# Padded broadcast matmuls, C copied among the gelus, a plain scan product, expert products in pairs and a router that normalizes in token order

## The chip, the cores and the metric

One core of a Trainium2 chip runs the whole program. The metric is the device time of one execution in microseconds, as the median of several runs; a lower number is better. Five engines work side by side and meet only at semaphores: TensorE (PE in the profile, with its weight loads as PEld), VectorE (DVE), ScalarE (ACT), GpSimd (POOL) and SyncE (SP), whose queue issues most of the transfers.

## The reference

The input is a batch of 16 images of 64 channels and 256 pixels. Three blocks follow one another, each added to its input. All of it is fp32.

```python
x = x + conv_block(group_norm(x))            # small graph convolution, done once in the prologue
t = tokens(x)                                # 16 x 256 tokens of 64 channels
# selective scan, state 16, inner width 128
z, gate = split(layer_norm(t) @ W_in + b_in)
xc = silu(z @ W_conv + b_conv)
Bp, Cp = split(xc @ W_bc + b_bc)
dt = softplus(xc @ W_dt + b_dt)
h[t] = exp(dt * A) * h[t-1] + dt * xc * Bp ;  y[t] = sum_over_state(h[t] * Cp)
t = t + (y * silu(gate)) @ W_out + b_out
# 8 experts, the best 2 of each token
n = layer_norm(t)
logits = n @ Wr + br ;  weights = top2(softmax(logits)), normalized to sum 1
xe = layer_norm(n) * ln_g[e] + ln_b[e]
out = sum_e weight[e] * (gelu(xe @ W1[e] + b1[e]) @ W2[e] + b2[e])
t = t + out
```

## The kernel before, in words

The 16 images are taken as 8 groups of two images (the two halves of the 128 partitions), so a tile is 128 partitions by 512 tokens. After a prologue (loads, weights brought into shape, group norm, the convolution), a body runs 8 times; a tail then finishes the last group. Body `i` scans group `i` (slots 0 to 7), starts the next two groups (`nxt`, `nxt2`: projections, `dt`, the `B` and `C` products), and finishes the group before (`prev`: output projection, layer norm, router, experts). Every engine has its instructions in an order written by hand, and semaphores say when each may start.

A slot is two blocks of 512 steps. VectorE forms the product of B and the broadcast input `ub` in PSUM (`dve_slot`, line 765), then runs the scan into `hs` (line 772). GpSimd multiplies `hs` by `Cs` (`pool_slot`, line 343), TensorE sums over the state (`pe_sum`, line 1059). After slot 0 of the next body, VectorE gates the sum (`dve_gate`, line 793): this text calls its start the **gate** and counts a body from one gate to the next.

Around slot 1 VectorE finishes the group before: `t1` (line 797), then, once slot 1's scan has been issued, `dve_lnF` (line 803, normalized tokens `tns` for the router), `dve_xn2` (lines 810 and 818, the experts' input) with the first router operations between, and `dve_router2` (lines 834 to 855, about ten operations on 128 x 32 or 128 x 4 elements). Meanwhile GpSimd does slot 0, `step_input` for the next group (lines 328 and 330, 128 x 512 each), slot 1, then `pool_x2` (line 368, the low part of the experts' input), which TensorE needs for the first expert matmul, then five small router operations.

The experts run on TensorE and ScalarE as a chain of eight pairs: matmuls by `W1` (lines 1195, 1196), gelu (line 638), matmuls by `W2` (line 1209). Four broadcasts of the router's weights over the partitions (`pe_wb`, line 1183) are copied to SBUF by ScalarE (line 631). VectorE multiplies each expert's result (bias column added) by its weight (`dve_expert`, line 863, 128 x 256), two after each of slots 4 to 7, and GpSimd adds them up (`pool_acc`, line 355).

## Time and profile before

| what | value |
|---|---|
| median of 3 runs | 400.92 us (400.79 to 401.01) |
| profiled execution | 399.73 us, of which the span of the trace is 398.0 us |
| busy in the span: TensorE, VectorE, ScalarE, GpSimd | 329.9, 333.5, 279.3, 266.2 us |
| prologue and body 0, to the first gate | 94.1 us |
| bodies, gate to gate (7) | 39.0, 38.8, 38.8, 38.8, 38.7, 38.5, 36.9 us |
| tail, from the last gate | 34.5 us |

Busy time is a sum over the span. The three stages have different limits, so what a change is worth is read from the stage that it is in. In the timeline views the first column is the start in us from the start of the span, the second the duration in us.

### The profile page before, as it was taken

What the parts mean: (1) busy time and instruction counts of PE and PEld (TensorE: products, weight loads), DVE (VectorE), ACT (ScalarE), POOL (GpSimd) and SP (SyncE); (2) the same over time, 40 slices, a digit from 0 to 9 for tenths busy, and PEclk for the clock granted to TensorE, in tenths of its full rate; (3) what the DMA queues carried; (4) which work ended last, traced back from release to release, by engine and by line L of the source; (5) the groups of instructions that cost most, each with busy time, mean ns of one, the idle gap of its engine ahead of it and who ended that gap; (6) DMA issues with size and microseconds to landing.
All of it is one profiled execution on the core that took longest, in us unless ns stands there. A gap on an engine that the chain in (4) does not pass through costs nothing. (4 is left out here: it accounts for less than half of the span.)

```text
span 398.0 us, 5484 instructions
## 1 busy us (share of the span) xinstructions
PE 329.9 (83%) x1658; PEld 176.3 (44%) x1658; DVE 333.5 (84%) x454; ACT 279.3 (70%) x458; POOL 266.2 (67%) x270
## 2 busy tenths in 40 slices
...
DMA packets 21236, 59.52 MB, mean 150 GB/s; under 512 B 4924, under 2 KB 13272, under 8 KB 15320
## 3 DMA queue, kind: packets, MB, share of 16 engines
...
q8 instruction: 13, 0.21, 0.3%
...
## 5 line engine op out<-in xcount | busy, mean ns | idle before, releaser
L343 POOL TENSOR_TENSOR hs<-hs,Cs 128x1024 f32<-128x1024 f32 x63 | 149.3, 2373 | 41.8 <-DVE hs L772 41.1
L772 DVE TENSOR_TENSOR_SCAN hs<-av,P 128x1024 f32<-128x1024 f32 x64 | 146.3, 2286 | 4.3 <-POOL av L336 1.3
L638 ACT ACTIVATE hb<-P,b1c 128x512 f32<-128x512 f32 x128 | 81.6, 684 | 17.8 <-PE P L1196 15.3
L765 DVE SCALAR_TENSOR_TENSOR P<-P,bbcol,ub 128x1024 f32<-128x1024 f32 x62 | 79.7, 1285 | 2.5 <-DMA ub<-u_scratch 1.2
L1209 PE MATMUL P<-hb,W2s 128*64 128x256 f32 x512 | 68.7, 391 | 0.0
L1195 PE MATMUL P<-X,W1H 128*128 128x512 f32 x128 | 60.4, 472 | 4.6 <-ACT hb L638 3.7
L1196 PE MATMUL P<-X,W1L 128*128 128x512 f32 x128 | 52.5, 410 | 0.0
L581 ACT ACTIVATE av<-P,Aneg 128x510 f32<-128x510 f32 x68 | 44.1, 688 | 9.4 <-PE P L1148 5.7
L355 POOL TENSOR_TENSOR accs<-accs,mes 128x256 f32<-128x256 f32 x56 | 41.0, 733 | 14.1 <-DVE mes L863 9.5
L1209 PEld LDWEIGHTS P<-hb,W2s 128*64 128x64 f32 x512 | 31.3, 136 | 30.6 <-issue 20.7
L863 DVE SCALAR_TENSOR_TENSOR mes<-P,cols,wbs 128x256 f32<-128x256 f32 x64 | 27.3, 468 | 16.0 <-PE P L1209 9.6
L1148 PE MATMUL P<-D,selD 128*128 128x512 f32 x64 | 33.0, 539 | 6.8 <-ACT av L581 4.3
L581 ACT ACTIVATE av<-av,Aneg 128x510 f32<-128x510 f32 x60 | 38.2, 707 | 0.1
L1195 PEld LDWEIGHTS P<-X,W1H 128*128 128x128 f32 x128 | 25.3, 198 | 27.8 <-ACT hb L638 16.7
L1059 PE MATMUL P<-hs,selS 128*32 128x512 f32 x256 | 30.6, 598 | 5.9 <-POOL hs L343 5.9
L631 ACT ACTIVATE wbs<-P 128x512 f32<-128x512 f32 x32 | 19.1, 598 | 20.7 <-PE P L1183 20.7
L1196 PEld LDWEIGHTS P<-X,W1L 128*128 128x128 f32 x128 | 25.7, 200 | 2.7
L1225 PE MATMUL P<-W1H 128*128 128x512 f32 x53 | 18.2, 449 | 5.2 <-POOL X L368 5.2
L1148 PEld LDWEIGHTS P<-D,selD 128*128 128x128 f32 x64 | 12.2, 196 | 20.7 <-issue 20.3
L1059 PEld LDWEIGHTS P<-hs,selS 128*32 128x32 f32 x256 | 6.8, 109 | 28.0 <-POOL hs L343 15.4
L1183 PE MATMUL P<-wT,selW 32*128 32x256 f32 x64 | 16.1, 330 | 0.0
L360 POOL TENSOR_TENSOR D<-dts,D 64x512 fp32r<-64x512 f32 x8 | 10.1, 1269 | 7.5 <-ACT D L564 6.7
...
## 6 DMA issues: line engine op xcount, KB each, us to landing
...
```

Source lines behind the costliest of these rows:

```text
L343: gp.tensor_tensor(hs[:, at, :, :], hs[:, at, :, :], rep(Cs[:, p, :], 1, 2), ALU.mult).then_inc(S["cm"], 1)
L355: gp.tensor_tensor(acc[:, p, :], prev, mes[:, e % 4, :], ALU.add).then_inc(S["acc"], 1)
L581: a_.activation(steps, dt_of, ACT.Exp, scale=Aneg[:, m:m + 1]).then_inc(S["aexp"], 1)
L638: a_.activation(hb[:, r % 4, :], P[:, (XA, XB)[r % 2], :], ACT.Gelu, bias=b1c[:, r:r + 1]).then_inc(S["gl"], 1)
L765: v.scalar_tensor_tensor(out=ring, in0=rep(P[:, BB, :], 1, 2), scalar=bbcol[:, 0:1], in1=ub[:, 2 * n:2 * n + 2, :], op0=ALU.add, op1=ALU.m ...
L772: v.tensor_tensor_scan(hs[:, (SLOTS * g + n) % RING].rearrange("p a t -> p (a t)"), av[:, 2 * n:2 * n + 2, :].rearrange("p a t -> p (a t)" ...
L863: v.scalar_tensor_tensor(out=mes[:, e % 4, :], in0=P[:, (XC, XD)[e // 2 % 2], HW * (e % 2):HW * (e % 2) + HW], scalar=cols[:, R["b2"] + e: ...
L1059: last = pe.matmul(P[32 * q:32 * q + 32, YS, :], selS[:, k, :], hs[:, (SLOTS * g + n) % RING, q % 2, :], start=(k == 0), stop=(k == 3))
L1148: pe.matmul(P[:, (YS, XA)[m % 2], :], selD[:, m - BY_PE[0], :], D2[:, :], start=True, stop=True).then_inc(S["dt_pe"], 1)
L1195: pe.matmul(P[:, bank, :], W1H[:, e, 128 * k:128 * k + 128], X2[:, :], start=True, stop=False)
L1196: pe.matmul(P[:, bank, :], W1L[:, e, 128 * k:128 * k + 128], X2[:, :], start=False, stop=True).then_inc(S["f1"], 1)
L1209: last = pe.matmul(P[64 * h:64 * h + 64, (XC, XD)[pair % 2], HW * (e % 2):HW * (e % 2) + HW], W2s[:, e, k, :], hb[:, r % 4, HW * h:HW * h ...
```

## The change

Seven edits that touch all five engines:

- **Broadcasts:** `selW` and `wT` get 128 partitions instead of 32 (rows above 32 are zero), so line 1183's matmuls contract over 128 rows.
- **C:** its matmul and its copy to `Cs` move from among the decays to the start of the experts' part, after the second pair of gelus.
- **Scan product:** B's bias goes into PSUM by a matmul of its own (`bhl` by `ones`); line 765 becomes a plain product without a scalar operand.
- **Expert products:** two experts at a time, 128 x 512, on VectorE and GpSimd; a last GpSimd addition folds the two halves.
- **Expert bias:** the weighted sum of `b2` comes from two matmuls per group (`pe_bias`); ScalarE copies it beside `t1`.
- **Logits:** `t1` is multiplied by a centred router matrix `Wrc` at once; `tns`, its two ScalarE operations of 128 x 256 and the bias matmul go.
- **Router norm:** the variance comes per token (`pe_vartok`) as 128 x 4; VectorE scales the logits by it and adds the bias, two operations of 128 x 32, ahead of `dve_xn2`.

In the tail the experts keep the old single form. Four buffers of the prologue move into `mes`.

```diff
...
-        selW = sb("selW", [32, EXP, 128], f32r)
+        selW = sb("selW", [128, EXP, 128], f32r)
...
+        bhl = sb("bhl", [128, ST * BLK], f32r)
+        ones = sb("ones", [128, 64], f32r)
...
-        wT = sb("wT", [32, HW], f32r)
+        wT = sb("wT", [128, HW], f32r)
...
+            sp_.wait_ge(S["k_b2"], 1)
+            for h in range(2):
+                for r in range(2):
+                    sp_.dma_start(b2f[16 * h + EXP * r:16 * h + EXP * r + EXP, 64 * h:64 * h + 64], b2).then_inc(S["ld_b2"], 16)
...
+        def pool_pair(eng, g, p, r):
+
+            eng.wait_ge(S["me"], EXP * g + 2 * r + 2)
+            if r == 0:
+                since(eng, "out_sem", 32 * g)
+                eng.wait_ge(S["bt"], g + 1)
+                prev = t1[:, p:p + 2, :]
+            else:
+                eng.wait_ge(S["acc"], EXP * g + 2 * r)
+                prev = acc[:, :, :]
+            at = 2 * (r % 2)
+            done = gp.tensor_tensor(acc[:, :, :], prev, mes[:, at:at + 2, :], ALU.add)
+            if r < EXP // 2 - 1:
+                done.then_inc(S["acc"], 2)
+            else:
+                done.then_inc(S["acc"], 1)
+                eng.wait_ge(S["acc"], EXP * g + EXP - 1)
+                gp.tensor_tensor(acc[:, 0, :], acc[:, 0, :], acc[:, 1, :], ALU.add).then_inc(S["acc"], 1)
...
+            gp.memset(b2f[:, :], 0.0).then_inc(S["k_b2"], 1)
...
+            gp.memset(bhl[:, :].bitcast(fp32), 0.0).then_inc(S["bhl"], 1)
+            gp.memset(ones[:, :].bitcast(fp32), 1.0).then_inc(S["bhl"], 1)
+            gp.memset(wT[:, :].bitcast(fp32), 0.0).then_inc(S["k_wt"], 1)
...
+            eng.wait_ge(S["ld_b2"], 64)
+            gp.tensor_copy(b2h[:, 0, :], b2f[:, :]).then_inc(S["b2r"], 1)
+            eng.wait_ge(S["b2r"], 1)
+            gp.tensor_tensor(b2h[:, 1, :], b2f[:, :], b2h[:, 0, :], ALU.subtract).then_inc(S["b2r"], 1)
...
-            a_.activation(rs2[:, :], P[:, XB, HW:T], ACT.Ln, bias=epst[:, 0:1]).then_inc(S["ln2"], 1)
+            eng.wait_ge(S["vt"], g + 1)
+            a_.activation(rv[:, 6], P[:, XC, 4 * EXP:4 * EXP + 4], ACT.Ln, bias=epst[:, 0:1]).then_inc(S["ln2"], 1)
...
-            a_.activation(rs2[:, :], rs2[:, :], ACT.Exp, scale=-0.5).then_inc(S["rs2"], 1)
+            a_.activation(rv[:, 7], rv[:, 6], ACT.Exp, scale=-0.5).then_inc(S["rs2"], 1)
...
+        def act_bias(eng, g):
+            eng.wait_ge(S["bt_mm"], g + 1)
+            since(eng, "acc", EXP * (g - 1) + 2)
+            a_.activation(t1[:, 1, :], P[:, XD, HW:T], ACT.Copy).then_inc(S["bt"], 1)
...
                 act_decay(eng, i, 10)
                 if prev is not None:
                     act_lnF2(eng, prev)
-                if nxt is not None:
-                    act_c(eng, nxt, q)
                 act_decay(eng, i, 11)
                 if nxt2 is not None:
                     act_lnA1(eng, nxt2)
-                act_decay(eng, i, 12, 13)
                 if prev is not None:
                     act_router(eng, prev)
+                act_decay(eng, i, 12, 13)
                 if nxt2 is not None:
                     act_lnA2(eng, nxt2)
                 act_decay(eng, i, 14, 15)
                 if prev is None:
                     act_dhi(eng, nxt)
+                    act_c(eng, nxt, q, YS)
                 if prev is not None:
                     a_.preload_act_table_set("gelu_and_others")
                     for n in range(EXP):
                             act_dhi(eng, nxt)
                         if n == 1:
                             act_wt(eng, prev)
+                            if nxt is not None:
+                                act_c(eng, nxt, q, YS)
+                        if n == 2:
+                            act_bias(eng, prev)
                         if n in range(2, 6):
                             act_wb(eng, prev, n - 2)
...
-                v.scalar_tensor_tensor(out=ring, in0=rep(P[:, BB, :], 1, 2), scalar=bbcol[:, 0:1], in1=ub[:, 2 * n:2 * n + 2, :],
-                                       op0=ALU.add, op1=ALU.mult).then_inc(S["bm"], 1)
+                v.tensor_tensor(ring, rep(P[:, BB, :], 1, 2), ub[:, 2 * n:2 * n + 2, :], ALU.mult).then_inc(S["bm"], 1)
...
-        def dve_lnF(eng, g):
-            eng.wait_ge(S["rs2"], g + 1)
-            since(eng, "lg", 2 * g)
-            v.tensor_tensor(tns[:, :], P[:, XB, 0:HW], rs2[:, :], ALU.mult).then_inc(S["tn"], 1)
-
-        def dve_xn2(eng, g, between=None):
+        def dve_xn2(eng, g):
...
-            logits = P[:, XC, 0:4 * EXP].rearrange("p (c e) -> p c e", e=EXP)
-            eng.wait_ge(S["lg"], 2 * (g + 1))
+            logits = rt[:, 2]
+            eng.wait_ge(S["rs2"], g + 1)
+            eng.wait_ge(S["lg"], g + 1)
+            v.tensor_tensor(rt[:, 0], P[:, XC, 0:4 * EXP].rearrange("p (c e) -> p c e", e=EXP), rep(rv[:, 7], 2, EXP), ALU.mult).then_inc(S["lm"], 1)
+            eng.wait_ge(S["lm"], 2 * g + 1)
+            v.tensor_tensor(logits, rt[:, 0], rep(brs[:, :], 1, 4), ALU.add).then_inc(S["lm"], 1)
+            eng.wait_ge(S["lm"], 2 * g + 2)
             v.tensor_reduce(rv[:, 0], logits, AX, ALU.max).then_inc(S["m1"], 1)
...
+        def dve_mes(eng, g, r):
+
+            eng.wait_ge(S["f2"], EXP * KC * g + 2 * KC * (r + 1))
+            eng.wait_ge(S["wb"], EXP // 2 * g + r + 1)
+            since(eng, "acc", EXP * g + 2 * (r - 1))
+            at = 2 * (r % 2)
+            v.tensor_tensor(mes[:, at:at + 2, :].rearrange("p e f -> p (e f)"), P[:, (XC, XD)[r % 2], :],
+                            wbs[:, 2 * r:2 * r + 2, :].rearrange("p e f -> p (e f)"), ALU.mult).then_inc(S["me"], 2)
...
+            v.tensor_copy(bhl[0:1, :], bbx[0:1, :, :].rearrange("p s e -> p (s e)")).then_inc(S["bhl"], 1)
+            eng.wait_ge(S["bhl"], 3)
+            v.tensor_tensor(bhl[32:33, :], bbx[0:1, :, :].rearrange("p s e -> p (s e)"), bhl[0:1, :], ALU.subtract).then_inc(S["bhl"], 1)
...
-                    dve_lnF(eng, prev)
+                    dve_router1(eng, prev)
                     dve_xn2(eng, prev)
                     dve_router2(eng, prev, nxt2)
...
+            pe.matmul(P[:, BB, :], bhl[:, :], rep(ones[:, :], 1, T // 64), start=True, stop=False)
             eng.wait_ge(S["xc"], g + 1)
-            since(eng, "bm", SLOTS * g)
-            pe.matmul(P[:, BB, :], Wrep[:, 0].rearrange("p s e -> p (s e)"), xc[:, g % 2, :], start=True, stop=True).then_inc(S["b_mm"], 1)
-
-        def pe_c(eng, g, bank=XC):
-            if bank == XC:
-                eng.wait_ge(S["sg"], g + 1)
+            pe.matmul(P[:, BB, :], Wrep[:, 0].rearrange("p s e -> p (s e)"), xc[:, g % 2, :], start=False, stop=True).then_inc(S["b_mm"], 1)
...
-            eng.wait_ge(S["cs"], so_far(g, 3))
-            pe.matmul(P[:, XC, 0:4 * EXP], ident[:, :], rep(brs[:, :], 1, 4), start=True, stop=False).then_inc(S["lgb"], 1)
-            eng.wait_ge(S["tn"], g + 1)
+            eng.wait_ge(S["t1"], g + 1)
+            eng.wait_ge(S["wrc"], 1)
             for q in range(2):
-                pe.matmul(P[:, XC, 2 * EXP * q:2 * EXP * q + 2 * EXP], tns[:, 128 * q:128 * q + 128],
-                          Wrt[:, :, :].rearrange("p h e -> p (h e)"), start=False, stop=(q == 1)).then_inc(S["lg"], 1)
+                last = pe.matmul(P[:, XC, 2 * EXP * q:2 * EXP * q + 2 * EXP], t1[:, 2 * (g % 2), 128 * q:128 * q + 128],
+                                 Wrc[:, :, :].rearrange("p h e -> p (h e)"), start=True, stop=True)
+            last.then_inc(S["lg"], 1)
+
+        def pe_vartok(eng, g):
+            eng.wait_ge(S["sq2"], g + 1)
+            for q in range(2):
+                last = pe.matmul(P[:, XC, 4 * EXP + 2 * q:4 * EXP + 2 * q + 2], sq2[:, 128 * q:128 * q + 128],
+                                 avg_m[:, 0:128:64], start=True, stop=True)
+            last.then_inc(S["vt"], 1)
...
+        def pe_bias(eng, g):
+
+            eng.wait_ge(S["wtc"], g + 1)
+            eng.wait_ge(S["b2r"], 2)
+            for r in range(2):
+                last = pe.matmul(P[:, XD, HW:T], b2h[:, r, :], wT[:, :], start=(r == 0), stop=(r == 1))
+            last.then_inc(S["bt_mm"], 1)
...
                     since(eng, "me", EXP * prev)
+                    pe_router(eng, prev)
                     pe_warm(eng, 2, XD)
                     pe_varF(eng, prev)
+                    pe_vartok(eng, prev)
                 pe_spread(eng, i, 11)
-                if nxt is not None:
-                    pe_c(eng, nxt)
                 pe_spread(eng, i, 12)
                 if nxt2 is not None:
                     pe_cenA(eng, nxt2)
-                if prev is not None:
-                    pe_router(eng, prev)
                 pe_spread(eng, i, 13)
                 if nxt2 is not None:
                     pe_varA(eng, nxt2)
                 pe_spread(eng, i, 15)
                 if prev is not None:
                     eng.wait_ge(S["xl2"], prev + 1)
-                    pe_warm(eng, 2, XB)
+                    pe_warm(eng, 1 if nxt is not None else 2, XB)
+                if nxt is not None:
+                    pe_c(eng, nxt)
+                if prev is not None:
                     pe_pair(eng, prev, 0)
                     pe_f1(eng, prev, 2)
                     pe_f1(eng, prev, 3)
                     pe_f2(eng, prev, 1)
                     for n in range(2, 6):
                         pe_pair(eng, prev, n)
+                        if n == 2:
+                            pe_bias(eng, prev)
                         pe_wb(eng, prev, n - 2)
...
```

The order on VectorE in body 1, from slot 1's scan product to the first operation of `dve_router2` (`rt`, `rv`: the router's scratch tiles; `tns`: normalized tokens; `X`: the experts' input), before:

```order
L765 SCALAR_TENSOR_TENSOR P<-P,bbcol,ub 128x1024 [waits scan]
L772 SCALAR_TENSOR_TENSOR hs<-av,P 128x1024 [waits ysum,aexp,bm]
L803 TENSOR_TENSOR tns<-P,rs2s 128x256 [waits rs2]
L810 TENSOR_TENSOR xnt<-P,rqs 64x256 [waits rq]
L810 TENSOR_TENSOR xnt<-P,rqs 64x256
L818 TENSOR_TENSOR X<-P,rqs 64x256
L823 TENSOR_REDUCE rv<-P 128x4 [waits lg]
L826 TENSOR_TENSOR rt<-P,rv 128x32 [waits m1]
L818 TENSOR_TENSOR X<-P,rqs 64x256
L834 SCALAR_TENSOR_TENSOR P<-P,rank 128x32 [waits ex]
```

and now:

```order
L811 TENSOR_TENSOR P<-P,ub 128x1024 [waits scan]
L817 SCALAR_TENSOR_TENSOR hs<-av,P 128x1024 [waits ysum,aexp,bm]
L860 TENSOR_TENSOR rt<-P,rv 128x32 [waits lg,rs2]
L862 TENSOR_TENSOR rt<-rt,brs 128x32 [waits lm]
L864 TENSOR_REDUCE rv<-rt 128x4 [waits lm]
L867 TENSOR_TENSOR rt<-rt,rv 128x32 [waits m1]
L850 TENSOR_TENSOR xnt<-P,rqs 64x256 [waits rq]
L850 TENSOR_TENSOR xnt<-P,rqs 64x256
L854 TENSOR_TENSOR X<-P,rqs 64x256 x2
L875 SCALAR_TENSOR_TENSOR P<-P,rank 128x32 [waits ex]
```

One 128 x 256 operation (`tns`) has gone, two of 128 x 32 have come, and the first four router operations stand ahead of the experts' input instead of within it.

The order on GpSimd from slot 7 of one body to `pool_x2` of the next (`accs`: the experts' sum; `dts`, `rl`: `dt` and the scan's input), before:

```order
L343 TENSOR_TENSOR hs<-hs,Cs 128x1024 [waits scan]
L355 TENSOR_TENSOR accs<-accs,mes 128x256 [waits acc,me] x2
L343 TENSOR_TENSOR hs<-hs,Cs 128x1024 [waits cs,scan]
L328 TENSOR_TENSOR dts<-rl,sp 128x512 [waits dt_out,dlo,sp_relu,sp_ln]
L330 TENSOR_TENSOR rl<-dts,xc 128x512 [waits dt]
L343 TENSOR_TENSOR hs<-hs,Cs 128x1024 [waits scan]
L368 TENSOR_TENSOR X<-xnt,X 64x512 [waits cm,acc,xh2,xn2]
```

and now:

```order
L352 TENSOR_TENSOR hs<-hs,Cs 128x1024 [waits scan]
L366 TENSOR_TENSOR accs<-accs,mes 128x512 [waits acc,me]
L372 TENSOR_TENSOR accs<-accs 128x256 [waits acc]
L352 TENSOR_TENSOR hs<-hs,Cs 128x1024 [waits cs,scan]
L337 TENSOR_TENSOR dts<-rl,sp 128x512 [waits dt_out,dlo,sp_relu,sp_ln]
L339 TENSOR_TENSOR rl<-dts,xc 128x512 [waits dt]
L352 TENSOR_TENSOR hs<-hs,Cs 128x1024 [waits scan]
L396 TENSOR_TENSOR X<-xnt,X 64x512 [waits cm,acc,xh2,xn2]
```

Two additions of 128 x 256 have become one of 128 x 512 and a fold; what follows them is unchanged.

The order on TensorE in the same stretch of body 1, behind the centred `t1` (`sq2s`: its square; line 1137, now 1197: its variance; `W1H`: fillers), before:

```order
L1133 MATMUL P<-t1s,cen_m 128x256 [waits t1]
L1148 MATMUL P<-D,selD 128x512 [waits aexp,dlo]
L1225 MATMUL P<-W1H 128x512 [waits xn1]
L1225 MATMUL P<-W1H 128x512
L1137 MATMUL P<-sq2s,avg_m 128x256 [waits sq2]
L1148 MATMUL P<-D,selD 128x512 [waits aexp,dlo]
L1120 MATMUL P<-xc,Wrep 128x512 [waits t1,sg]
L1148 MATMUL P<-D,selD 128x512 [waits aexp,dlo]
L1065 MATMUL P<-res,cen_m 128x256
L1163 MATMUL P<-brs,ident 128x32 [waits cs]
L1166 MATMUL P<-Wrt,tns 128x16 [waits tn]
L1166 MATMUL P<-Wrt,tns 128x16
```

and now:

```order
L1193 MATMUL P<-t1s,cen_m 128x256 [waits t1]
L1208 MATMUL P<-D,selD 128x512 [waits aexp,dlo]
L1225 MATMUL P<-Wrc,t1s 128x16 [waits wrc,t1,xn1]
L1225 MATMUL P<-Wrc,t1s 128x16
L1302 MATMUL P<-W1H 128x512 x2
L1197 MATMUL P<-sq2s,avg_m 128x256 [waits sq2]
L1232 MATMUL P<-avg_m,sq2s 128x2 [waits sq2]
L1232 MATMUL P<-avg_m,sq2s 128x2
L1208 MATMUL P<-D,selD 128x512 [waits aexp,dlo] x2
```

The two router matmuls (lines 1166, now 1225) have moved from behind `tns` to ahead of the variance, and the variance per token (line 1232) stands behind it; C's matmul (line 1120) has left the stretch.

## Rows read from the trace of the kernel before

**Rows 1.** Windows, one body: stretch, length, busy PE, PEld, DVE, ACT, POOL, clock, DMA

```profile
171.80:210.60 38.80, 34.49 (x182) 17.45 (x182) 37.31 (x46) 33.67 (x57) 30.98 (x28) 1.00 0.79 181
```

**Rows 2.** Timeline of VectorE, the body that begins at 210.60

```profile
210.60 0.69 DVE L793 TENSOR_TENSOR ygs<-P,sg 128x512 f32<-128x512 f32 x1 [0.18 <-PE P L1059]
...
213.76 2.29 DVE L772 TENSOR_TENSOR_SCAN hs<-av,P 128x1024 f32<-128x1024 f32 x1
215.97 0.42 DVE L803 TENSOR_TENSOR tns<-P,rs2s 128x256 f32<-128x256 f32 x1
216.31 0.86 DVE L810 TENSOR_TENSOR xnt<-P,rqs 64x256 f32<-64x256 f32 x2
...
217.98 0.19 DVE L826 TENSOR_TENSOR rt<-P,rv 128x32 f32<-128x32 f32 x1
...
218.95 0.20 DVE L834 SCALAR_TENSOR_TENSOR P<-P,rank 128x32 f32<-128x32 f32 x1 [0.32 <-ACT P L620]
...
221.06 1.28 DVE L765 SCALAR_TENSOR_TENSOR P<-P,bbcol,ub 128x1024 f32<-128x1024 f32 x1
```

**Rows 3.** Timeline of GpSimd, the same body

```profile
209.38 1.60 POOL L355 TENSOR_TENSOR accs<-accs,mes 128x256 f32<-128x256 f32 x2
...
214.65 1.27 POOL L330 TENSOR_TENSOR rl<-dts,xc 128x512 f32<-128x512 f32 x1
216.13 2.36 POOL L343 TENSOR_TENSOR hs<-hs,Cs 128x1024 f32<-128x1024 f32 x1 [0.21 <-DVE hs L772]
218.76 1.27 POOL L368 TENSOR_TENSOR X<-xnt,X 64x512 fp32r<-64x512 f32 x1 [0.28 <-DVE X L818]
```

**Rows 4.** Timelines of GpSimd and VectorE, the last body

```profile
334.74 1.26 POOL L368 TENSOR_TENSOR X<-xnt,X 64x512 fp32r<-64x512 f32 x1 [0.23 <-POOL hs L343]
...
335.58 0.47 DVE L846 TENSOR_TENSOR rt<-rt,rv 128x32 f32<-128x32 f32 x1
```

**Rows 5.** Timelines of the prologue: VectorE, GpSimd, SyncE's queue

```profile
11.55 1.57 DVE L882 TENSOR_TENSOR gdev<-mv,gmean 128x8 f32<-128x8 f32 x1
...
13.54 2.09 POOL L440 TENSOR_TENSOR ub<-av 128x256 f32<-128x256 f32 x3 [0.44 <-DMA av<-in_L_conv_Wr]
...
20.22 0.29 SPq L302 DMA_DIRECT2D ub<-in_L_ffn_ln_b  x1
...
29.03 3.69 POOL L447 TENSOR_TENSOR wbs<-hb,cols 128x2048 f32<-128x2048 f32 x1 [11.14 <-DMA hb<-in_L_ffn_W]
...
29.37 3.39 DVE L944 TENSOR_SCALAR Aneg<-Aexp 128x16 f32<-128x16 f32 x1
```

**Rows 6.** Timelines of ScalarE and TensorE around the router, body at 210.60

```profile
214.79 0.47 ACT L589 ACTIVATE rs2s<-P,epst 128x256 f32<-128x256 f32 x1 [0.21 <-PE P L1137]
...
214.82 1.02 PE L1120 MATMUL P<-xc,Wrep 128*128 128x512 f32 x2
...
217.12 0.60 PE L1166 MATMUL P<-Wrt,tns 128*128 128x16 f32 x4
```

**Rows 7.** VectorE groups by line and form: busy, mean ns | idle before

```profile
L760 DVE TENSOR_TENSOR P<-P,hs 128x1024 f32<-128x1024 f32 x2 | 2.5, 1233 | 4.2 <-PE P L1159 4.2
```

**Rows 8.** Timeline of VectorE, a pair of expert products after slot 4

```profile
197.48 0.85 DVE L863 SCALAR_TENSOR_TENSOR mes<-P,cols,wbs 128x256 f32<-128x256 f32 x2
```

**Rows 9.** Timelines of ScalarE and VectorE, slot 7 ahead of the gate at 210.60

```profile
205.24 1.33 ACT L581 ACTIVATE av<-av,Aneg 128x510 f32<-128x510 f32 x2
...
208.14 2.29 DVE L772 TENSOR_TENSOR_SCAN hs<-av,P 128x1024 f32<-128x1024 f32 x1
```

**Rows 10.** Timeline of TensorE in the tail

```profile
382.00 0.50 PE L1183 MATMUL P<-wT,selW 32*128 32x256 f32 x2
382.43 0.51 PE L1195 MATMUL P<-X,W1H 128*128 128x512 f32 x1
382.77 0.40 PE L1196 MATMUL P<-X,W1L 128*128 128x512 f32 x1
```

**Rows 11.** Line 846 in all bodies: ns of the shortest, the median, the longest

```profile
L846 DVE TENSOR_TENSOR rt<-rt,rv x8: 180/182/465, 104.0 to 373.4; 128x32 f32<-128x32 f32 x8
```

More of the change, by code:

```diff
@@ L59 @@
 bm scan cm ysum
-yg po t1 cen2 sq2 var2 ln2 rs2 lnq rq tn xn2 xh2 xl2
-lg lgb m1 dd ex s1 ms1 o1 e2 m2 s2 s2r ms2 o2 den rden num wt wn vhi vlo wtr wtc wb_mm wb
+yg po t1 cen2 sq2 var2 ln2 rs2 lnq rq xn2 xh2 xl2
+lg vt lm wrc m1 dd ex s1 ms1 o1 e2 m2 s2 s2r ms2 o2 den rden num wt wn vhi vlo wtr wtc ld_b2 k_b2 b2r bt_mm bt wb_mm wb
 f1 gl f2 me acc out_sem""".split()
@@ L164, in build @@
         ygs = sb("ygs", [128, T])
-        t1 = sb("t1s", [128, 2, HW])
+        t1 = sb("t1s", [128, 3, HW])
+        b2h = sb("b2h", [128, 2, 128], f32r)
         sq2 = sb("sq2s", [128, HW])
-        rs2 = sb("rs2s", [128, HW])
         rqs = sb("rqs", [128, HW])
-        tns = sb("tns", [128, HW])
         xnt2 = sb("xnt2", [64, T])
@@ L465, in weighted @@
                     if prev is not None:
-                        for e in range(lo, lo + 2):
-                            pool_acc(eng, prev, q, e)
+                        pool_pair(eng, prev, q, lo // 2)
                 if i == 0:
@@ L603, in act_lnF2 @@
             eng.wait_ge(S["var2"], g + 1)
-            since(eng, "tn", g)
+            since(eng, "dd", g)
             since(eng, "xn2", 2 * g)
@@ L719, in _ @@
             eng.wait_ge(S["b_mm"], 1)
-            a_.activation(B0, P[:, BB, :], ACT.Identity, bias=bbcol[:, 0:1]).then_inc(S["b0"], 1)
+            a_.activation(B0, P[:, BB, :], ACT.Copy).then_inc(S["b0"], 1)
             act_lnA1(eng, 1)
@@ L810, in dve_xn2 @@
                 v.tensor_tensor(xnt2[:, HW * h:HW * h + HW], P[q, XB, 0:HW], rqs[q, :], ALU.mult).then_inc(S["xn2"], 1)
-            if between is not None:
-                between()
             since(eng, "f1", EXP * KC * g)
@@ L815, in dve_xn2 @@
                 q = slice(64 * h, 64 * h + 64)
-                if h == 1 and between is None:
-                    dve_router1(eng, g)
                 v.tensor_tensor(X2[0:64, HW * h:HW * h + HW], P[q, XB, 0:HW], rqs[q, :], ALU.mult).then_inc(S["xh2"], 1)
         def dve_router1(eng, g):
-            logits = P[:, XC, 0:4 * EXP].rearrange("p (c e) -> p c e", e=EXP)
-            eng.wait_ge(S["lg"], 2 * (g + 1))
+            logits = rt[:, 2]
[5 more added lines that the diff above has]
+            eng.wait_ge(S["lm"], 2 * g + 2)
             v.tensor_reduce(rv[:, 0], logits, AX, ALU.max).then_inc(S["m1"], 1)
@@ L1132, in pe_cenF @@
             since(eng, "gl", EXP * KC * g)
-            pe.matmul(P[:, XB, 0:HW], cen_m[:, :], t1[:, p, :], start=True, stop=True).then_inc(S["cen2"], 1)
+            pe.matmul(P[:, XB, 0:HW], cen_m[:, :], t1[:, 2 * p, :], start=True, stop=True).then_inc(S["cen2"], 1)
         def pe_varF(eng, g):
```

62 lines of the change are left out of this document (41 added, 21 removed).

## Prediction

> **What bounds the kernel now.** First the windows of one body, then VectorE's and GpSimd's timelines inside it. In 38.80 us from gate to gate VectorE is busy 37.31, TensorE 34.49, ScalarE 33.67, GpSimd 30.98 [rows 1]. VectorE's row has only two gaps that its neighbours cause: 0.18 us at the gate, where TensorE's sum of slot 7 comes late, and 0.32 us ahead of the router's first masked operation (line 834), which waits for ScalarE's exponentials [rows 2]. So seven bodies go at VectorE's pace, and a change is worth there what it adds to or takes from VectorE's chain between two gates. I count from the gate at 210.60: slot 1's scan starts at +3.16, its next operation at +5.37, and slot 2's product, P(2), at +10.46 [rows 2].
>
> At the gate GpSimd arrives last: after slot 7's second pair of additions (1.60 us) it is directly in slot 0's product, then `dt` and `u`, then slot 1's product at +5.53, then `pool_x2`, which ends at +9.43 and releases the experts [rows 3].
>
> **A wait that the trace already has.** In the last body one small VectorE operation, line 846 (128 x 32, both inputs in SBUF), took 0.47 us from 335.58 and ended at 336.05. GpSimd's `pool_x2` ran from 334.74 to 336.00 [rows 4]. Line 826 is of the same size with one input in PSUM, ran from 217.98, in the middle of GpSimd's slot 1 (216.13 to 218.49), and took 0.19 [rows 2, 3]. The prologue repeats it: line 882 (both inputs in SBUF, 128 x 8) took 1.57 and ended at 13.12, as GpSimd's copies ended (13.54 less the 0.44 idle: 13.10); line 944 (another form, all in SBUF) took 3.39 and ended at 32.76, GpSimd's line 447 ended at 32.72 [rows 5]. I read: such a VectorE operation stands still until GpSimd has an idle moment. The Trainium skill, "SBUF — State Buffer", section "Who interferes with whom", states it so: a VectorE instruction with two SBUF inputs contends with a GpSimd instruction that reads SBUF, and whichever starts first holds the shared ports to its end, while one with at most one SBUF input does not contend. The rows agree, and the rule speaks against this change.
>
> **The change in a body.** The new `dve_router1` has two operations of that kind where there was none: line 862 (logits plus `brs`) and line 867 (less the maximum; its first input was in PSUM before). Both stand directly behind slot 1's scan, where GpSimd hardly rests.
>
> When does it begin? Before, ScalarE's first operation on the variance started at 214.79 [rows 6]. Now two router matmuls stand ahead of the variance (0.60 for the old pair [rows 6]) and two more behind it, while ScalarE's two operations per token shrink to four columns. I put `rs2` at +5.85, 0.5 behind the scan.
>
> When is GpSimd busy? Its last pair now costs 1.27 (the duration of 128 x 512 in `u`) plus a fold of 0.80 (half of the 1.60) against 1.60, so +0.47. Of that the 0.21 idle ahead of slot 1 [rows 3] takes some: slot 1 runs from about +5.85 to +8.2.
>
> So line 862 reaches the port as that product begins, and waits to +8.27. Then the maximum, and line 867 ends at +8.7. Experts' input: two of 0.43 and two of 0.43 (1.73 in all [rows 2]), to +10.4; by then the exponentials are ready, and the 0.32 wait is gone. Behind it `dve_router2` takes 2.11 as now (218.95 to 221.06 [rows 2]): P(2) at +12.44 instead of +10.46, **+1.98**. The 0.42 of `tns` and two small operations are in this sum. `pool_x2` ends 2.33 later, at +11.76.
>
> **What the body gets back.** The product without the scalar operand: the only plain 128 x 1024 product with one PSUM input in the trace took 1233 ns [rows 7], line 765 takes 1.28 [rows 2], so 0.05 each. A pair of expert products: 0.85 for two of 128 x 256 [rows 8]; one of 128 x 512 from PSUM takes 0.69 (line 793 [rows 2]), so 0.16 each. To slot 5's scan that is four products and one pair, **-0.36**. From there the later chain is GpSimd's, since it is what the gate waits for: two pairs from 1.60 to 1.28 each, **-0.64** (VectorE saves as much there: three pairs 0.48, three products 0.15). Sum per body +1.98 - 0.36 - 0.64 = **+0.98**, times 7 = **+6.9**. Bounds: line 862 gets into the pause between `u` and slot 1 (then only line 867 waits, +1.53 instead of +1.98), or neither waits (5.85 + 0.7 for four small operations + 1.73 + 2.11 = +10.39, so -0.07).
>
> **Experts.** C's matmul (1.02 [rows 6], less one filler dropped, 0.24) now stands ahead of the first expert matmul, its copy and the bias copy among the gelus (my estimate 0.47 for both, part of them in ScalarE's waits): with `pool_x2` the experts come 2.33 + 0.78 + 0.47 = 3.6 later. Before, the last decays ended at 206.57, 1.57 ahead of slot 7's scan [rows 9], and that scan itself now comes 1.98 - 0.30 (six products) - 0.48 (three pairs) = 1.2 later: 2.8 may be lost. So the sides are level if the broadcasts save 0.8. A broadcast pair with 32 rows, two of 256 columns, takes 0.43 from its start to the next; the expert matmul of 512 columns and 128 rows behind it takes 0.34 [rows 10]. Of the two the operand with fewer rows is the dearer, so I let padding halve the broadcasts: four times 0.2, and this part costs nothing. Without the saving it costs 0.8 a body if every term adds, 0.35 if the copies hide behind gelus. The Trainium skill, "TensorE: Matmul & The Clock Gate", section "Why this matters for your kernels", speaks against the saving: a single matmul with K = 32 takes the same time as one with K = 128. No row here has both shapes at one width, so that is a rival below.
>
> **Ends.** Prologue: about 0.64 us of new fills on GpSimd (my estimate for their 128 x 512 elements and some more, between 0.2 and 1) close the 0.44 pause ahead of line 440 in which line 882 got through, so it falls behind line 440 (2.09 [rows 5]), up to +2.7 on the group norm. Four more transfers on SyncE's queue at 0.3 [rows 5] delay line 447 by 1.2, and what waits behind it on VectorE (line 944). These overlap: I take **+2.0**, bounds +0.2 (both beside other loads) and +3. Body 0: six products, **-0.2**. Tail: router's two operations +0.44, later variance +0.4, `tns` -0.34, broadcasts down to -0.8 that mostly hide behind gelus: **+0.1**.
>
> **Sum.** 2.0 - 0.2 + 6.9 + 0.1 = +8.8. The profiled execution took 399.73, 1.2 below the median, so 408.5 in a profile and **409.7** as a median.
>
> **Rivals.**
> - *No wait (faster).* If a 128 x 32 operation gets its inputs between GpSimd's reads, P(2) comes at +10.4 and a body gains 1.07: 7 x -1.07 + 1.9 (the ends) = -5.6, **395.3**. For it: line 846 took 0.18 as a median [rows 11]; against: in the body of rows 2 and 3 it ran after `pool_x2`, with GpSimd idle, and the instance with GpSimd at work took 0.47. It decides where P(2) comes less than 0.73 later (7 x -0.27 + 1.9 = 0). Chance 0.14.
> - *One of two waits.* Line 862 slips into the pause ahead of slot 1; +0.53 a body, 3.7 + 1.9 = +5.6: **406.5**. Chance 0.14.
> - *The experts become the bound.* Padding saves nothing; the decays of slot 7 come late by 0.6, between 0.35 and 0.8, and a body costs 1.58: x 7 + 1.9 = +13.0, **413.9**. Chance 0.14.
> - My forecast: 0.54. The last 0.04 is a mixture near zero.
>
> Measurement of this kernel tells apart about 0.2%. The forecast and the two middle rivals are slower, the first rival faster: faster 0.15, same 0.03, slower 0.82. The likeliest case alone spans 407.5 (prologue at its lower bound) to 411.5. The range goes to 404.0, between the partial wait and a body that hides part of it, and to 414.5 for the experts' case.
>
> **What would show it.** Lines 862 and 867 with about 2 us between them instead of 0.2 each, one ending as GpSimd's slot 1 (now line 352) ends; P(2) at gate + 12.4; bodies of about 39.8; pairs of products at 0.69, products at 1.23, additions at 1.28; broadcasts at 0.2 to 0.25 a pair. If lines 862 and 867 take 0.19 in the bodies, the forecast is wrong in sign. If they wait but bodies are no longer, another engine already set P(2).

## Result, and the profile after

| what | before | changed |
|---|---|---|
| median of 6 runs | 400.97 us | 414.32 us (411.61 to 415.78) |
| ratio, 95% interval | | 1.0324 (1.0302 to 1.0347) |
| profiled execution, span | 399.73, 398.0 us | 411.61, 409.9 us |
| first gate | 94.1 us | 96.9 us |
| gate to gate (7) | 39.0, 38.8, 38.8, 38.8, 38.7, 38.5, 36.9 us | 40.7, 39.4, 40.4, 40.3, 39.4, 39.6, 38.4 us |
| tail, from the last gate | 34.5 us | 34.8 us |

The kernel is 3.2% slower. Of the 11.9 us in the span, 2.8 come before the first gate, 8.9 in the seven bodies, 0.3 in the tail. The profiled execution is the fastest of the six, 2.7 us below their median. Ahead of the last body, three bodies take 39.4 to 39.6 and three 40.3 to 40.7. One of the four executions in experiment 5 below took 1021.92 us, for a reason that no row shows, and the ratio there leaves it out.

The timeline of VectorE in the body that begins at 177.01 (start, duration, operation), for comparison with [rows 2]:

```profile
183.06 0.19 DVE L860 TENSOR_TENSOR rt<-P,rv 128x32 f32<-128x32 f32 x1 [0.66 <-ACT rv L633]
183.29 1.89 DVE L862 TENSOR_TENSOR rt<-rt,brs 128x32 f32<-128x32 f32 x1
...
185.44 0.19 DVE L867 TENSOR_TENSOR rt<-rt,rv 128x32 f32<-128x32 f32 x1
...
189.46 1.23 DVE L811 TENSOR_TENSOR P<-P,ub 128x1024 f32<-128x1024 f32 x1
```

and of GpSimd, for [rows 3]:

```profile
175.79 1.28 POOL L366 TENSOR_TENSOR accs<-accs,mes 128x512 f32<-128x512 f32 x1
177.16 0.73 POOL L372 TENSOR_TENSOR accs<-accs 128x256 f32<-128x256 f32 x1
...
182.78 2.35 POOL L352 TENSOR_TENSOR hs<-hs,Cs 128x1024 f32<-128x1024 f32 x1
187.45 1.26 POOL L396 TENSOR_TENSOR X<-xnt,X 64x512 fp32r<-64x512 f32 x1 [2.32 <-DVE X L854]
```

Line 862 is as small as line 860, which has its first input in PSUM and takes 0.19. It takes 1.89 and ends at 185.18; GpSimd's slot 1 ends at 185.13. No wait is shown in brackets: the engine counts as busy while it stands. Behind it everything is late: P(2), line 811, starts 12.45 behind the gate instead of 10.46, and `pool_x2` (line 396) ends at +11.70 instead of +9.43; GpSimd, which held VectorE up, then idles 2.32 waiting for it. In the whole trace:

```profile
L862 DVE TENSOR_TENSOR rt<-rt,brs x8: 191/1454/1941, 103.0 to 383.1; 128x32 f32<-128x32 f32 x8
```

(shortest, median, longest, in ns). The shortest is that of the tail, where GpSimd is idle.

The savings are there too, in the groups by line and form (busy us, mean ns of one):

```profile
L811 DVE TENSOR_TENSOR P<-P,ub 128x1024 f32<-128x1024 f32 x62 | 76.0, 1226 | 2.7 <-DMA ub<-u_scratch 0.7
L366 POOL TENSOR_TENSOR accs<-accs,mes 128x512 f32<-128x512 f32 x21 | 27.0, 1285 | 2.4 <-DVE mes L914 2.4
L914 DVE TENSOR_TENSOR mes<-P,wbs 128x512 f32<-128x512 f32 x28 | 18.6, 666 | 0.0
```

**Why two kinds of body.** Windows of two bodies, and of the stretch from +10 to +16 in each (length, busy PE, PEld, DVE, ACT, POOL, then the granted clock as a share of full speed):

```profile
257.69:297.07 39.38, 33.86 (x186) 17.79 (x186) 36.67 (x43) 33.95 (x60) 30.18 (x24) 1.00 0.76 172
177.01:217.44 40.43, 35.06 (x186) 18.64 (x186) 37.93 (x43) 32.45 (x57) 31.60 (x26) 0.96 0.78 176
267.69:273.69 6.00, 4.57 (x18) 2.40 (x20) 5.73 (x16) 5.59 (x10) 2.68 (x7) 1.00 1.01 220
187.01:193.01 6.00, 4.47 (x10) 2.42 (x10) 5.76 (x15) 4.23 (x8) 2.46 (x6) 0.72 1.01 223
```

In the longer one TensorE runs for some time at 0.50, the lower of its two levels (1.2 GHz), just when the experts should begin. Its timeline there shows what it did before and during the fall:

```profile
186.61 1.05 PE L1208 MATMUL P<-D,selD 128*128 128x512 f32 x2 [1.60 <-ACT av L616]
188.76 0.80 PE L1302 MATMUL P<-W1H 128*128 128x512 f32 x1 [1.10 <-POOL X L396]
189.36 1.91 PE L1180 MATMUL P<-xc,Wrep 128*128 128x512 f32 x2
```

Two pauses, 1.60 for ScalarE's decays (ScalarE waits for the router, line 867, ahead of them) and 1.10 for `pool_x2`; then C's matmul takes 1.91, against 1.02 at full clock [rows 6]. The pauses alone do not tell which body has the fall: they are 0.44 and 1.12 in the body at 257.69, which kept full clock, and 0.45 and 1.11 in a body of experiment 6 (at 258.27) which did not and took 40.89 instead of 39.38. Why the clock falls in one and not in the other stays open. What the fall costs is seen at the body's end, on VectorE:

```profile
214.96 2.29 DVE L817 TENSOR_TENSOR_SCAN hs<-av,P 128x1024 f32<-128x1024 f32 x1 [0.75 <-PE P L1115]
```

The next body's first scan waits for TensorE's sums (line 1115), which stand behind the experts in TensorE's queue. The bodies at 96.89 and 177.01 have this wait of 0.75, that at 217.44 one of 0.84 for ScalarE's decays; those at full clock wait only 0.26, at the gate. The sixth body, of 39.6, had a fall too (0.56 in the mean from +10 to +16) without such a wait; it has no `nxt2` to start. The body of before that begins at 210.60 has a fall of the clock too, and the same length as the others:

```profile
210.60:249.37 38.77, 35.73 (x182) 18.18 (x182) 37.33 (x47) 33.42 (x56) 30.95 (x28) 0.96 0.78 179
```

There VectorE waits 0.18 at the gate and at most 0.1 in the 27 us ahead of it. I read: there the experts' slack paid for the fall, and `pool_x2`, 2.0 to 2.3 later, has used that slack up.

### The profile page after: what moved, and what is told of

Its sections match the earlier page's. It is cut to its first block and busy times, and to the rows that moved or that the text cites. A ratio compares the mean times of both kernels' runs of the same rounds, so it can differ in the third digit from the quotient of the medians.

```text
span 409.9 us, 5566 instructions
## 1 busy us (share of the span) xinstructions
PE 336.8 (82%) x1691; PEld 185.8 (45%) x1691; DVE 331.3 (81%) x437; ACT 274.5 (67%) x465; POOL 267.8 (65%) x255
## 5 line engine op out<-in xcount | busy, mean ns | idle before, releaser
L811 DVE TENSOR_TENSOR P<-P,ub 128x1024 f32<-128x1024 f32 x62 | 76.0, 1226 | 2.7 <-DMA ub<-u_scratch 0.7
L1272 PE MATMUL P<-X,W1L 128*128 128x512 f32 x128 | 53.4, 417 | 0.0
L1208 PE MATMUL P<-D,selD 128*128 128x512 f32 x64 | 29.9, 514 | 25.6 <-ACT av L616 23.7
L1208 PEld LDWEIGHTS P<-D,selD 128*128 128x128 f32 x64 | 12.2, 206 | 40.1 <-issue 39.8
L366 POOL TENSOR_TENSOR accs<-accs,mes 128x512 f32<-128x512 f32 x21 | 27.0, 1285 | 2.4 <-DVE mes L914 2.4
L1302 PE MATMUL P<-W1H 128*128 128x512 f32 x46 | 16.7, 462 | 7.2 <-POOL X L396 7.2
L396 POOL TENSOR_TENSOR X<-xnt,X 64x512 fp32r<-64x512 f32 x7 | 8.8, 1264 | 16.2 <-DVE X L854 16.2
L914 DVE TENSOR_TENSOR mes<-P,wbs 128x512 f32<-128x512 f32 x28 | 18.6, 666 | 0.0
L904 DVE SCALAR_TENSOR_TENSOR mes<-P,cols,wbs 128x256 f32<-128x256 f32 x8 | 3.5, 480 | 16.1 <-PE P L1286 8.8
```

The lines of the kernel that those rows point to most:

```text
L366: done = gp.tensor_tensor(acc[:, :, :], prev, mes[:, at:at + 2, :], ALU.add)
L811: v.tensor_tensor(ring, rep(P[:, BB, :], 1, 2), ub[:, 2 * n:2 * n + 2, :], ALU.mult).then_inc(S["bm"], 1)
L1208: pe.matmul(P[:, (YS, XA)[m % 2], :], selD[:, m - BY_PE[0], :], D2[:, :], start=True, stop=True).then_inc(S["dt_pe"], 1)
L1272: pe.matmul(P[:, bank, :], W1L[:, e, 128 * k:128 * k + 128], X2[:, :], start=False, stop=True).then_inc(S["f1"], 1)
L1302: pe.matmul(P[:, bank, :], W1H[:, 0, 0:128], W1H[:, 0:2, :].rearrange("p e f -> p (e f)"), start=True, stop=True)
```

## Experiments

Ratios are to the kernel before on the same chip, with the 95% interval.

**1. The two router tiles in PSUM (e1_psum).** Only the place of two tiles changes.

```diff
+        scaled = P[:, XC, 160:160 + 4 * EXP].rearrange("p (c e) -> p c e", e=EXP)
+        biased = P[:, XC, 192:192 + 4 * EXP].rearrange("p (c e) -> p c e", e=EXP)
...
-            logits = rt[:, 2]
+            logits = biased
...
-            v.tensor_tensor(logits, rt[:, 0], rep(brs[:, :], 1, 4), ALU.add).then_inc(S["lm"], 1)
+            v.tensor_tensor(logits, scaled, rep(brs[:, :], 1, 4), ALU.add).then_inc(S["lm"], 1)
```

> Two intermediate tiles of the router (scaled logits, logits with bias) lie in PSUM instead of SBUF, so that neither line 862's nor line 867's counterpart has two inputs in SBUF; number, size and order of all operations stay. Theory (the wait is for GpSimd, because of two SBUF inputs): both operations take 0.19 to 0.2 us, P(2) comes at gate + 10.5 to 10.8 instead of 12.2 to 12.45, pool_x2 ends 1.5 earlier, bodies of 37.8 to 38.3, time 398 to 402. Rival (what holds P(2) is the late variance rs2 and the order of the operations): P(2) stays at + 11.5 or later and the time above 409.

399.1 us, ratio 0.9949 (0.9928 to 0.997): 15 us less than the changed kernel. VectorE's and GpSimd's timelines in one body (line 864 was 862):

```profile
179.90 0.20 DVE L864 TENSOR_TENSOR P<-P,brs 128x32 f32<-128x32 f32 x1
```

```profile
179.38 2.36 POOL L354 TENSOR_TENSOR hs<-hs,Cs 128x1024 f32<-128x1024 f32 x1
```

It now runs in 0.20 in the middle of GpSimd's slot 1. Ahead of the last body P(2) comes at +10.6 to +11.6, later than expected where the variance is late (the counterpart of line 860 starts at +5.9 to +6.9); these bodies take 37.9 to 38.8, up to 0.5 more than expected.

**2. One operation added to the kernel before (e5_ss, e6_ps).** Unused output, directly behind line 803; the second kernel differs in one input.

```diff
             v.tensor_tensor(tns[:, :], P[:, XB, 0:HW], rs2[:, :], ALU.mult).then_inc(S["tn"], 1)
+            v.tensor_tensor(rt[:, 2], rank[:, :, :], rank[:, :, :], ALU.add)
```

```diff
+            v.tensor_tensor(rt[:, 2], P[:, XB, 0:4 * EXP].rearrange("p (c e) -> p c e", e=EXP), rank[:, :, :], ALU.add)
```

> The kernel before with one operation more per group on VectorE, directly behind line 803: 128 x 32, both inputs the constant tile rank in SBUF, output unused. Nothing waits for it but VectorE's own order. Theory (it stands still until GpSimd's product of slot 1 has ended): it takes 1.8 to 2.2 us in the bodies, P(2) comes 1.5 to 2.0 later and pool_x2 2 later, bodies longer by 1.2 to 2.5 (nothing is given back here), time 408 to 418. Rival (small operations slip through): it takes 0.2, time 401 to 402.5.

> The same added operation with one of its two inputs in PSUM (the centred tokens, in a bank that is free to read there), otherwise the kernel before. Theory: 0.2 us, P(2) 0.1 to 0.2 later, time 401 to 402.5. Rival (any added operation here costs a stall): as the other kernel.

Two inputs in SBUF: 414.28 us, 1.034 (1.0294 to 1.0386). One in PSUM: 400.54 us, 1.0001 (0.9973 to 1.003). The added line in all groups of the first and of the second:

```profile
L804 DVE TENSOR_TENSOR rt<-rank x8: 183/1777/2226, 100.3 to 382.8; 128x32 f32<-128x32 f32 x8
```

```profile
L804 DVE TENSOR_TENSOR rt<-P,rank x8: 180/180/181, 99.6 to 369.4; 128x32 f32<-128x32 f32 x8
```

The first brings P(2) to +12.1, `pool_x2`'s end to +11.35, the bodies to 40.3 to 40.6, all but the last, with TensorE at 0.50 to 0.72 in the mean from +10 to +16: the changed kernel's picture, from one operation of 0.18 us, eight times. Seven of the eight wait (the one in the tail takes 0.18), and this costs nearly 14 us, about as much as the whole change.

**3. Router behind the experts' input (e3_swap).**

```diff
-                    dve_router1(eng, prev)
                     dve_xn2(eng, prev)
+                    dve_router1(eng, prev)
```

> VectorE does the experts' input ahead of the four router operations again, otherwise the changed kernel. Theory (waits end with GpSimd's product of slot 1, whatever stands there): pool_x2 ends at about + 9.6 instead of 11.8, and now one of the two operations with two SBUF inputs stands behind pool_x2 instead (0.5 to 1.3 us); P(2) at + 11.7 to 12.2, no fall of the clock, bodies of 39.0 to 39.4, time 407 to 410. Rival (the wait belongs to the operations themselves, not to GpSimd): line 862 still takes 1.5 to 1.9 and pool_x2 is as early, P(2) at 12.2 or later. If nothing waits: bodies below 38.5, time below 403.

422.86 us, 1.0534 (1.0487 to 1.058). The wait went where it was expected, the time did not. VectorE and GpSimd:

```profile
230.33 1.18 DVE L862 TENSOR_TENSOR rt<-rt,brs 128x32 f32<-128x32 f32 x1
```

```profile
230.21 1.26 POOL L396 TENSOR_TENSOR X<-xnt,X 64x512 fp32r<-64x512 f32 x1 [1.06 <-DVE X L854]
```

Line 862 now ends with `pool_x2` (231.51 and 231.47): the wait went to GpSimd's next operation. `pool_x2` itself ended 1.0 to 2.2 earlier. But line 867 came at +10.5 here, and ScalarE has the exponentials that wait for it ahead of four decays and of the next group's normalization, for which line 823 then waited 0.90; in the first five bodies P(2) came at +13.3 to +14.3 and they took 41.5 to 42.4. The clock, which was expected to stay, fell in all bodies. I had counted only VectorE's queue.

**4. More for TensorE to do (e2_fill, e7_keep).**

```diff
                 pe_spread(eng, i, 15)
+                    eng.wait_ge(S["aexp"], NBLK * i + 15)
+                    pe_warm(eng, 10, YS)
```

> Ten more filler matmuls on TensorE between the last spread of a body and the wait for the experts' input, nothing else. Theory A (bodies of 40.2 to 40.7 differ from those of 39.4 because TensorE's clock falls while it waits for pool_x2, and the experts have no slack left): the granted clock stays at 1.00 behind gate + 9, all middle bodies at 39.3 to 39.5, time 409 to 411. Rival (the experts are late by C's matmul and the copies, whatever the clock): bodies keep their spread, time 414 or more.

422.81 us, 1.0525 (1.0475 to 1.0575), and no answer: the fillers waited for a late decay, began at +11.2, when the clock had fallen already, took 5.06 us for eleven and stood in the experts' way. Better placed:

```diff
+                    pe_warm(eng, 4, XD)
                 if nxt2 is not None:
                     pe_cenA(eng, nxt2)
...
+                    eng.wait_ge(S["xh2"], 2 * (prev + 1))
+                    pe_warm(eng, 5, XB)
                     eng.wait_ge(S["xl2"], prev + 1)
```

> The changed kernel with nine more filler matmuls per body on TensorE, where it waits anyway: four ahead of line 1121, into a bank that nobody reads then, and five between the experts' high part and pool_x2's end. Theory (what bodies of 40.2 to 40.9 have above those of 39.4 is TensorE's clock, granted at half from about gate + 10): the clock stays at 1.00, P(2) stays at 12.2, and all middle bodies take 39.2 to 39.6, time 408 to 411. Rival (the longer bodies come from the experts' own lateness): bodies stay above 40 at a clock of 1.00.

409.99 us, 1.023 (1.0181 to 1.0278). Line 862 and P(2) (+12.2 to +12.5) are as in the changed kernel. Windows of two bodies:

```profile
175.55:214.94 39.39, 36.21 (x195) 19.41 (x195) 36.98 (x44) 33.72 (x59) 30.30 (x24) 1.00 0.76 173
135.13:175.55 40.42, 37.33 (x195) 20.56 (x195) 37.97 (x44) 32.52 (x57) 31.59 (x26) 0.96 0.83 189
```

Of the six bodies ahead of the last, five kept 1.00 and took 39.4 to 39.7; the one whose clock fell took 40.4. The ratio fell by 0.009, so some 4 us of the change's cost went with TensorE's clock.

**5. ScalarE's exponentials behind decays 12 and 13 again (e12_exp).**

```diff
-                if prev is not None:
-                    act_router(eng, prev)
                 act_decay(eng, i, 12, 13)
+                if prev is not None:
+                    act_router(eng, prev)
```

> The changed kernel with ScalarE's exponentials of the router behind decays 12 and 13 again, as in the kernel before; nothing else. Theory (while line 862 waits, ScalarE waits for the logits ahead of the decays, 1.4 us a body, and TensorE for these decays, and in that pause its clock falls): the exponentials come as early, decays 12 to 15 1.2 earlier, TensorE's pause ahead of the last two spreads goes, the clock stays at 1.00 in more bodies, these take 39.2 to 39.5; line 862's wait and P(2) stay at 12.2 to 12.5: time 408 to 412. Rival (the pause behind them, ahead of pool_x2's end, decides): clock and bodies as in the changed kernel, time 413 to 415.

Three executions of 409.57 to 415.34 us, 1.028 (1.0223 to 1.0337), not to be told from the changed kernel. The spreads came earlier and the pause ahead of the last two went, but TensorE's pause ahead of `pool_x2` grew from 1.1 to 1.9, and in the profile all bodies had the lower clock (the first five took 41.0 to 41.6, more than in the changed kernel). The rival came nearer: while `pool_x2` is late, the pause ahead of it stays, and the clock falls.

**6. The prologue (e4_pro).** Loads of `b2`, four fills and the two operations on `bhl` moved behind what others wait for.

```diff
-            sp_.wait_ge(S["k_b2"], 1)
-            for h in range(2):
-                for r in range(2):
-                    sp_.dma_start(b2f[16 * h + EXP * r:16 * h + EXP * r + EXP, 64 * h:64 * h + 64], b2).then_inc(S["ld_b2"], 16)
...
             sp_.dma_start(brs[:, :], rep(fbr, 0, 128)).then_inc(S["ld_dup"], 16)
+            sp_.wait_ge(S["k_b2"], 1)
+            for h in range(2):
+                for r in range(2):
+                    sp_.dma_start(b2f[16 * h + EXP * r:16 * h + EXP * r + EXP, 64 * h:64 * h + 64], b2).then_inc(S["ld_b2"], 16)
...
```

> Only the prologue's additions move: the four loads of b2 behind all other loads, the four fills on GpSimd to its pause before the experts' weights, VectorE's two operations on bhl behind the copy of selW. Theory: the first gate comes at 94 to 95 instead of 96.9, the rest stays, time 411.5 to 412.5. Rival (the prologue is longer because of the fp32 matmuls' clock or of other edits): first gate at 96 or later, time 413.5 or more.

413.19 us, 1.029 (1.025 to 1.0331). First gate 95.3 in this profile; over the profiles of all programs, six with the changed kernel's prologue have it at 95.0 to 96.9 (mean 95.9), four with this one at 94.0 to 95.4 (94.8), three with that of before at 93.7 to 94.4 (94.1). So the order of the additions is worth about 1.1 in the mean, though the ranges overlap; the time lies between theory and rival. The kernel before with padding alone (experiment 8), which adds one of the fills, has its gate at 95.0 in its one profile. In this profile all bodies had the lower clock and the first five took 40.6 to 40.9, four of them with the same P(2) (+12.2) as the 39.4 of the changed kernel:

```profile
176.67:217.42 40.75, 36.09 (x186) 19.23 (x186) 37.16 (x44) 33.18 (x58) 31.01 (x25) 0.92 0.76 173
```

**7. A version that beats both (e8_psum_pro_keep, e11_early).** Experiments 1 and 6, with fillers as in e7_keep, but:

```diff
-                    pe_warm(eng, 5, XB)
+                    pe_warm(eng, 4, XB)
                     eng.wait_ge(S["xl2"], prev + 1)
-                    pe_warm(eng, 1 if nxt is not None else 2, XB)
```

> Candidate: the changed kernel with both intermediate tiles of the router in PSUM, the prologue's additions behind the other loads, and the fillers (four and four, in place of the one ahead of C's matmul). Theory: the three add up, bodies of 37.7 to 38.6 at a clock of 1.00, first gate at 95, time 394 to 398, below both kernels. Rival (the fillers cost as much as the clock): time 398.5 or more.

396.39 us, 0.9895 (0.9852 to 0.9938), 1% below the kernel before, all bodies at 1.00, the first six of 37.9 to 38.4:

```profile
171.44:209.56 38.12, 35.69 (x193) 19.00 (x193) 36.16 (x44) 33.06 (x58) 30.95 (x25) 1.00 0.81 184
```

Then the two fillers ahead of the variance moved:

```diff
                     pe_router(eng, prev)
-                    pe_warm(eng, 2, XD)
                     pe_varF(eng, prev)
...
-                    pe_warm(eng, 4, XD)
+                    pe_warm(eng, 6, XD)
```

> e8_psum_pro_keep with the two fillers ahead of the variance (line 1197) moved behind it, to the four ahead of line 1121. Theory (P(2) now follows the variance: line 860's counterpart idles 0.6 to 1.1 for rs2): rs2 and P(2) 0.4 to 0.5 earlier, bodies 37.5 to 37.8, time 393 to 395. Rival (something else sets the gate, as the experts or GpSimd): bodies stay at 38.0, time 396 to 397.

397.39 us, 0.9914 (0.9884 to 0.9943): no gain. The variance came 0.4 to 0.6 earlier, but line 823's counterpart then waited 0.36 for the next group's normalization, and the gate stayed.

**8. Padding (e9_nopad, e10_padonly).** In e8's kernel the broadcasts take 32 rows again; in the kernel before they get 128.

```diff
-                pe.matmul(P[:, YS, HW * (e % 2):HW * (e % 2) + HW], selW[:, e, :], wT[:, :],
+                pe.matmul(P[:, YS, HW * (e % 2):HW * (e % 2) + HW], selW[0:32, e, :], wT[0:32, :],
```

> e8_psum_pro_keep with the four broadcast pairs per group contracting over 32 rows again, nothing else. Theory (a broadcast pair and the matmul behind it are 0.1 us dearer each where the number of rows changes between neighbours, 0.8 us a group): a pair takes 0.43 instead of 0.34 to the next start and that next one 0.34 instead of 0.24; the experts' part of e8's bodies has little slack, so 0 to 0.8 a body and 0.8 in the tail: time 397 to 402. Rival (the rows make no difference): both pitches stay, time 396.4.

> The kernel before with selW and wT padded to 128 rows, nothing else. Theory: the same 0.2 us per broadcast pair, hidden in the bodies of before behind VectorE and worth 0.3 to 0.8 in the tail: time 399.5 to 400.6 against 400.4. Rival (padding alone shortens the bodies): 395 or less.

Without padding 404.88 us, 1.009 (1.006 to 1.0119), more than expected. Padding alone 400.67 us, 1.0006 (0.9978 to 1.0035): in its profile six bodies are as before, the seventh is 0.5 and the tail 0.8 shorter, and the first gate comes 0.9 later. TensorE with 32 rows (e9) and with 128 (the changed kernel), two broadcasts and the matmuls behind them:

```profile
236.58 0.50 PE L1253 MATMUL P<-wT,selW 32*128 32x256 f32 x2
237.01 0.50 PE L1273 MATMUL P<-X,W1H 128*128 128x512 f32 x1
237.35 0.40 PE L1274 MATMUL P<-X,W1L 128*128 128x512 f32 x1
```

```profile
392.12 0.51 PE L1251 MATMUL P<-wT,selW 128*128 128x256 f32 x2
392.46 0.40 PE L1271 MATMUL P<-X,W1H 128*128 128x512 f32 x1
392.70 0.39 PE L1272 MATMUL P<-X,W1L 128*128 128x512 f32 x1
```

From start to start: 0.43 and 0.34 with 32 rows, 0.34 and 0.24 with 128, so 0.2 a pair, half of it on the neighbour. The weight loads of that neighbour, in the same order:

```profile
237.00 0.19 PEld L1273 LDWEIGHTS P<-X,W1H 128*128 128x128 f32 x1
```

```profile
392.35 0.19 PEld L1271 LDWEIGHTS P<-X,W1H 128*128 128x128 f32 x1
```

Behind 128 rows the load starts 0.11 ahead of its matmul, behind 32 rows only with it. The two broadcasts themselves, behind 64 columns, start 0.22 apart in both.

Without padding the profile's seven bodies together are 4.8 us longer than e8's (in the first five, the next body's first scan waits 0.57 to 0.68, which it does not in e8), the tail 1.6, and the first gate is 1.4 earlier. In the tail four pairs explain 0.8; the rest stands beside a longer stretch at the lower clock, and the tail of e11_early, which has the padding, is as long (36.8). So of the 7.8 us between the ratios I can place about 5.6; the rest stays open, and the profiled execution (401.68) is the fastest of its kernel.

## Why the prediction was right, and where it was off

- **The wait.** The step held. Forecast: line 862 stands to the end of slot 1, line 867 at +8.7, P(2) at +12.44, `pool_x2`'s end at +11.76. Measured: line 867 ends at +8.3 to +8.6, P(2) at +12.16 to +12.45, `pool_x2` at +11.4 to +11.7. Lines 862 and 867 never wait both, since GpSimd rests until `pool_x2`. The forecast's own terms do not quite add up: 8.7, 1.73 and 2.11 make 12.54, not 12.44. Experiments 1 and 2 show the cause, two inputs in SBUF against a running GpSimd operation, from both sides. This is what the Trainium skill, "SBUF — State Buffer", section "Who interferes with whom", says; the runs agree (1.78 against 0.18 us as medians of the added line). So VectorE and GpSimd do not meet only at semaphores, as the first section of this text has it.
- **What the body gets back.** Forecast 1.00 a body. A body at full clock (257.69) has P(2) 1.70 later and is 0.61 longer than before, so it got back 1.09. In e7_keep, with its fillers, the body at 214.94 has P(2) 1.98 later, as forecast, and is 0.90 longer at full clock, so 1.08 again. Of the forecast +0.98 a body, 0.61 to 0.90 came true.
- **The experts.** This is the step that was off: "this part costs nothing" held only at full clock. The forecast had the slack used up exactly (by its own terms even 0.2 short: the scan that it calls slot 7's is the next body's first, with seven products and four pairs ahead of it, so 1.0 and not 1.2 late). It did not ask what a fall of TensorE's clock, which the trace of before shows and which cost nothing there, then costs: 0.9 to 1.4 in the three longer bodies of the changed kernel, 1.2 to 1.5 in the first five of experiment 6. The sum for the bodies, +6.9, stands against +8.9 because that term was 0 and the others somewhat too dear: seven times 0.61 would have been 4.3, seven times 0.90 6.3. The six executions go with it at the ends only: a mean clock of 0.921 in the fastest (411.6), 0.893 in the slowest (415.8), and no order between.
- **The number.** The forecast of +8.8 stands against +13.4 between the medians. 414.32 lies 0.2 below the upper end of the range, which was put there for the rival with the experts as the bound; that rival's 413.9 is the nearest figure, but its reason, a padding that saves nothing, did not happen. That the median fell inside was luck in part.
- **Padding.** The 0.2 a pair was right, the reason not: not columns through fewer rows are dearer, but the change of shape between neighbours. Behind the pair the change costs the 0.1 and 0.1 above; ahead of the pair it shows where the matmul in front has 128 rows and columns (line 1261 in e9): the two broadcasts then start 0.22 apart with 32 rows, 0.12 with 128. So the right size was luck. The Trainium skill, "TensorE: Matmul & The Clock Gate", section "Why this matters for your kernels" (a single matmul takes as long with K = 32 as with 128), fits the matmul by itself, but in this sequence the measured 0.43 against 0.34 decides.
- **Prologue and body 0.** Forecast +1.8; +2.8 in this profile, +1.8 as a mean over the profiles (95.9 against 94.1). The mechanism was half wrong. Line 882 (now 932) did not fall behind GpSimd, it slipped in; VectorE and SyncE in the changed kernel:

```profile
11.85 0.17 DVE L932 TENSOR_TENSOR gdev<-mv,gmean 128x8 f32<-128x8 f32 x1
...
31.26 0.16 DVE L999 TENSOR_SCALAR Aneg<-Aexp 128x16 f32<-128x16 f32 x1
```

```profile
23.81 1.31 SPq L316 DMA_DIRECT2D hb<-in_L_ffn_W  x2
```

The loads of the experts' weights were issued at 23.81, 2.05 later, and line 999 no longer waits for GpSimd at all: it starts at 31.26, GpSimd's line 479 (447 before) at 31.46. Instead TensorE's small matmuls ended at 35.8 (32.3 before); before and in the changed kernel:

```profile
28.03 4.25 PE L1281 MATMUL P<-mu,av 128*128 128x16 f32 x36
```

```profile
29.52 6.26 PE L1358 MATMUL P<-mu,av 128*128 128x16 f32 x36
```

They began 1.5 later and took 2.0 more, with a granted clock of 0.71 from 30 to 33 and 0.50 from 33 to 36. In experiment 6 they took 4.17 at full clock, but there line 932 and the counterpart of line 999 stand again (1.46 and 3.60). All additions moved at once there, so what each is worth stays open.
- **Rivals.** "No wait" would have given 395.3; with the wait taken away it was 399.1: the variance is late, so P(2) comes at +10.6 to +11.6 and not at +10.4, and the clock still falls in four of its seven bodies. "The experts become the bound" happened in part, by the clock and not by the padding.
